# The sums over the experts of token tiles 1 and 3 move from VectorE to a tree of three additions on POOL

## What is computed

```python
logits = xt @ router_w + router_b
probs = jax.nn.softmax(logits, axis=-1)
gate = jnp.max(probs, axis=-1)
idx = jnp.argmax(probs, axis=-1)
out_all = jnp.einsum('th,ehd->ted', xt, expert_w) + expert_b[None, :, :]
e_out = jnp.take_along_axis(out_all, idx[:, None, None], axis=1)[:, 0, :]
y = gate[:, None] * e_out
...
x = _layernorm(x + _L0_ffn_ref(x, ...), axis=-1)
```

## Time and profile before

| | |
|---|---|
| median of three runs | 2217.35 us (2217.06 to 2220.44) |
| the profiled execution | 2223.95 us, of which the span is 2221.9 us |
| mean granted TensorE clock | 0.949 of full speed |
| PE / VectorE / ACT / POOL busy | 92% / 78% / 67% / 15% |
| sums over the experts on VectorE (L1470) | 32, 61.1 us |
| memsets of the attention's buffers on POOL in this stage | 20 (L640 4, L645 16), 36.7 us |

### The profile page before, as it was taken

One profiled execution on the slowest core, in us unless ns is written; L12 is line 12 of the kernel. 1 busy time (PEld: TensorE's weight loads), 2 busy tenths in 40 slices (PEclk: granted clock), 3 DMA queues, 4 the chain that ended last, 5 costly groups with the idle time before them and its releaser, 6 DMA issues.

```text
span 2221.9 us, 32029 instructions
## 1 busy us (share of the span) xinstructions
PE 2039.9 (92%) x10812; PEld 846.9 (38%) x10812; DVE 1737.5 (78%) x3501; ACT 1486.8 (67%) x2004; POOL 341.7 (15%) x385
## 2 busy tenths in 40 slices
PE   5748886999999999999999999999999999999995
PEld 2224443333333333444444444444444444443332
DVE  5856887788787877888888888888878888888884
ACT  4743453566666677777777777777777777776664
POOL 1101332000000011111111111111111111113223
PEclk9977786799999999999999999999999999999998
DMA  3001104233333355566566656556666566665630
GB/s 103 19 24 54 56 33 86 43 66 75 63 75 67 82 104 107 117 109 109 109 109 109 108 109 109 108 110 109 109 110 108 108 109 109 109 108 101 98 58 25
DMA packets 137197, 195.63 MB, mean 88 GB/s; under 512 B 20152, under 2 KB 55632, under 8 KB 137040
## 3 DMA queue, kind: packets, MB, share of 16 engines
q1 hardware_dynamic: 137040, 193.63, 45.5%
HBM read 75.45 MB, written 23.73 MB: 45 GB/s over the span
## 4 chain that ended last, share of the span: by engine, by line
PE 81%; DVE 13%; issue 4%; ACT 1%; POOL 1%; DMA 1%; DVEq 0%; POOLq 0%; SPq 0%; ACTq 0%
PE bank_s L1031 27%; PE bank_o L1069 22%; PE bank_x L1054 6%; DVE nm L1386 5%; PE bank_m L1082 3%; PE bank_x L1017 3%; PE bank_x L996 3%; PE bank_x L1004 2%; PE bank_m L1102 2%; PE bank_x L983 2%; PE bank_x L1128 2%; PE bank_s L934 1%; DVE big L1275 1%; PE bank_m L1092 1%; PE bank_m L1041 1%
## 5 line engine op out<-in xcount | busy, mean ns | idle before, releaser
L1386 DVE TENSOR_REDUCE nm<-bank_s 128x1 f32<-128x512 f32 x2048 | 1336.2, 685 | 342.3 <-PE bank_s L1031 341.4
L821 ACT ACTIVATE big<-bank_x 128x1024 f32<-128x1024 f32 x1024 | 1048.0, 1024 | 486.5 <-PE bank_x L1054 458.9
L1031 PE MATMUL bank_s<-kst,qst 62*128 62x512 f32 x2048 | 837.5, 469 | 53.1 <-DVE nm L1386 52.5
L1054 PE MATMUL bank_x<-qst,kst 64*128 64x512 f32 x2048 | 750.0, 447 | 1.6 <-ACT big L821 1.6
L1031 PEld LDWEIGHTS bank_s<-kst,qst 62*128 62x128 f32 x2048 | 358.9, 187 | 693.3 <-DVE nm L1386 609.4
L1069 PE MATMUL bank_o<-big,at 128*32 128x512 f32 x4096 | 556.4, 616 | 2.2 <-ACT big L821 2.0
L1054 PEld LDWEIGHTS bank_x<-qst,kst 64*128 64x128 f32 x2048 | 304.3, 187 | 10.2 <-issue 6.0
L605 POOL CAST at<-at 128x512 fp32r<-128x512 f32 x112 | 68.2, 609 | 1273.3 <-ACT at L752 1035.8
L607 POOL TENSOR_TENSOR at<-at 128x512 fp32r<-128x512 f32 x112 | 143.3, 1280 | 10.0
L1069 PEld LDWEIGHTS bank_o<-big,at 128*32 128x32 f32 x4096 | 81.2, 108 | 153.1 <-issue 149.2
L829 ACT ACTIVATE big<-bank_x,big 128x128 f32<-128x128 f32 x256 | 68.7, 376 | 27.3 <-issue 11.6
(11 more groups left out here) (154 smaller groups left out, 1511.4 us busy)
## 6 DMA issues: line engine op xcount, KB each, us to landing
at<-nodes_d SPq DMA_DIRECT2D x144, 256.0 KB, 5.9
kst<-at SPq DMA_DIRECT2D x288, 128.0 KB
qst<-at SPq DMA_DIRECT2D x288, 128.0 KB
nodes_d<-big SPq DMA_DIRECT2D x48, 256.0 KB, 3.1
at<-w_d SPq DMA_DIRECT2D x48, 193.0 KB, 5.8
at<-x2T_d SPq DMA_DIRECT2D x32, 256.0 KB, 4.4
kst<-at SPq DMA_DIRECT2D x128, 64.0 KB
qst<-at SPq DMA_DIRECT2D x128, 64.0 KB
```

Of the source, the lines that this page charges most:

```text
L821: act.activation(PT[:, kp, h, :, :], ring.take()[0].rearrange("p (c n) -> p c n", c=2), ACT.Exp, scale=x.c.scale).then_inc(S["c_ex"], 1)
L1031: pe.matmul(bank_s[:, n % 2, :], qst[rows, x.r, h, t * P:(t + 1) * P], kst[rows, x.r, h, :], start=True, stop=True).then_inc(S["c_s_ps"], 1)
L1054: mm = pe.matmul(sec(to, j), kst[rows, x.r, h, kc_ * P:(kc_ + 1) * P], qst[rows, x.r, h, :], start=True, stop=True)
L1386: dve.tensor_reduce(nm[:, k, at_n:at_n + 1], bank_s[:, n % 2, :], AX.X, ALU.max, negate=True).then_inc(S["c_red"], 1)
```

## The change

The sums of tiles 1 and 3 are taken from VectorE's queue. POOL does them in `scaled[1]`, in place, as a tree: 512 elements onto 512, 256 onto 256, and the last 128 onto 128 into `esum`, each addition waiting for the one before it. In POOL's queue, tile 3 of b2 comes first in an iteration, and tile 1 of b1 behind the reciprocal roots and ahead of the memsets and the split. L1412 waits for both engines' sums, and ACT's scaling of tiles 1 and 3 for POOL's. Tiles 0 and 2 stay on VectorE.

```diff
--- before.py
+++ after.py
@@ -227,8 +227,8 @@
               "ab", "ln", "sp", "mb_ps", "mb_ev", "dB_out", "link", "link2")
         names("r_", "A", "bx", "dA", "hs", "in", "out")
         names("b_", "x", "hs", "c_ps", "y", "yo_ps", "mv", "rs", "rs_link", "x1", "xT_ps", "xT_ev", "lg_ps", "lg", "ex", "mg", "mgT_ps",
-              "mgT_ev", "yb_ps", "acc", "e_ps", "sc", "red", "mv2", "rs2", "rs2_link", "x2", "x2T_ps", "x2T_ev", "out", "outT",
-              "link", "link2", "link3")
+              "mgT_ev", "yb_ps", "acc", "e_ps", "sc", "red", "red_odd", "mv2", "rs2", "rs2_link", "x2", "x2T_ps", "x2T_ev", "out", "outT",
+              "link", "link2", "link3", "tree")
         names("f_", "x3_in", "tT_ps", "tT_ev", "mv", "rs", "rs_link", "nm", "z", "mv2", "rs2", "rs2_link", "y", "out", "link", "link2", "plink")
         names("c_", "qk0", "qk1", "v0", "v1", "o0", "o1", "kh_ps", "qh_ps", "qT_ps", "v_ps", "ot_ps", "mT_ps", "wo_ps", "cT_ps", "x3T_ps",
               "kf_ev", "qf_ev", "q_ev", "v_ev", "ot_ev", "mT_ev", "pv_ev", "cT_ev", "wo_ev", "x3T_ev", "sp", "stk0", "stk1", "stk2",
@@ -622,6 +622,16 @@
                     pool.sem_inc(passed, 1)
                     in_parts(qf, qp, base + 1, S["c_sp"], 1)
 
+            def odd_sum(b, t):
+
+                of, m = scaled[1].rearrange("p e d -> p (e d)"), 2 * (2 * b + t // 2)
+                now(pool, "b_sc", b, NT, t + 1)
+                pool.tensor_tensor(of[:, 0:4 * D], of[:, 0:4 * D], of[:, 4 * D:8 * D], ALU.add).then_inc(S["b_tree"], 1)
+                pool.wait_ge(S["b_tree"], m + 2)
+                pool.tensor_tensor(of[:, 0:2 * D], of[:, 0:2 * D], of[:, 2 * D:4 * D], ALU.add).then_inc(S["b_tree"], 1)
+                pool.wait_ge(S["b_tree"], m + 3)
+                pool.tensor_tensor(esum[:, t * D:(t + 1) * D], of[:, 0:D], of[:, D:2 * D], ALU.add).then_inc(S["b_red_odd"], 1)
+
             def residual_rstd(x):
                 x = only(x, False)
                 if x is None or not x.half:
@@ -629,11 +639,14 @@
                 rstd(mv, rs0, rs, eps_ln[:, :], (S["c_mv"], x.b + 1), (S["c_plink"], x.b + 1), S["c_rs"])
 
             def body(b):
-                b2 = b - 2
+                b1, b2 = b - 1, b - 2
                 if batch(b2):
+                    odd_sum(b2, 3)
                     rstd(mvb, rsb0, rsb, eps_ln[:, :], (S["b_mv2"], b2 + 2), (S["b_rs2_link"], b2 + 2), S["b_rs2"])
                 if batch(b):
                     rstd(mva, rsa0, rsa, eps_ln[:, :], (S["b_mv"], b + 2), (S["b_rs_link"], b + 2), S["b_rs"])
+                if batch(b1):
+                    odd_sum(b1, 1)
                 if b in (2, 4, 6, 8):
                     r = b // 2 - 1
                     pool.wait_ge(S["b_y"], 2 * r + 3)
@@ -824,7 +837,7 @@
             def scale(b, t):
 
                 now(act, "b_e_ps", b, NT, t + 1)
-                need(act, S["b_red"], NT * b + t)
+                need(act, S["b_red_odd" if t % 2 else "b_red"], 2 * b + t // 2 + 1)
                 for e_ in range(NE):
                     i = act.activation(scaled[t % 2][:, e_, :], bank_x[:, t % 2, e_ * D:(e_ + 1) * D], ACT.Identity, scale=lgm[:, t, e_:e_ + 1])
                 i.then_inc(S["b_sc"], 1)
@@ -1399,15 +1412,13 @@
                     dve.tensor_scalar(nmx, mx, -1.0, None, ALU.mult).then_inc(S["b_lg"], 1)
                 if batch(b0):
                     with_d(b0, 0, A)
-                if batch(b2):
-
-                    expert_sum(b2, NT - 1)
                 if batch(b1):
                     before(dve, "b_mgT_ps", b1)
                     before(dve, "b_sc", b1, NT)
                     B.count(dve.tensor_tensor(lgm, lg, mx.unsqueeze(2).broadcast_to([P, NT, NE]), ALU.is_equal))
                 if batch(b2):
-                    now(dve, "b_red", b2, NT)
+                    now(dve, "b_red", b2, 2)
+                    now(dve, "b_red_odd", b2, 2)
                     now(dve, "b_acc", b2)
                     C.count(dve.tensor_tensor(tg[:, 1, :], tg[:, 1, :], esum, ALU.add))
                 if batch(b1):
@@ -1447,7 +1458,6 @@
                     before(dve, "b_out", b2, 16)
                     normalise(x2w, tg[:, 1, :], mvb, rsb, S["b_x2"])
                 if batch(b1):
-                    expert_sum(b1, 1)
                     now(dve, "b_yb_ps", b1)
                     before(dve, "b_x2", b1)
                     dve.tensor_tensor(tg[:, 1, :], bank_s[:, 0, :], hn, ALU.add).then_inc(S["b_acc"], 1)
```

## The result

The kernel after takes 2229.53 us (median of 5 runs, 2228.50 to 2232.94) against 2218.62 us for the kernel before (median of 5, 2217.06 to 2222.44). The ratio is 1.005, with a 95% interval of 1.0035 to 1.0064: slower by 10.9 us, or 0.5%. The profiled execution took 2229.15 us (span 2227.3).

The account below looks back on a forecast made before the run. Mostly VectorE's queue was taken to bound the expert stage, with TensorE's lower clock lengthening odd first halves. +0.6 + 9.0 - 10.4 + 6.1 = +5.3, with the clock +12.3 us, on the median 2217.35: 2229.6 us, range 2220.5 to 2238.

Parts of the forecast that it names:

- The removal: Expert stage: 16 of VectorE's 32 reductions go, 30.5 us of busy time, 30 us faster if all on the path.
- The tree: POOL's three dependent additions take 2.65 us, in latency 0.75 us longer than the reduction replaced.
- Tile 3, ordinary: First halves of b = 4 and 6: VectorE's addition of the sums waits for POOL, +0.3 us each, +0.6 together.
- Tile 3 behind the memsets: First halves of b = 3, 5, 7: tile 3's tree queues behind memsets delayed by tile 1's tree; +9.0 us.
- Tile 1 and the normalise: Second halves: VectorE reaches the normalise 1.9 us sooner, though POOL's additions hold it up; sum -10.4 us.
- two normalise instructions, second addition 0.74, the other two: end at +5.8: Second halves: the normalise, interleaved with tile 1's tree, ends 5.8 us after the mid-iteration addition.
- The end of the stage: Iterations b = 8 and 9: the last tile 1 tree delays memsets and split, and nothing covers it; +6.1 us.
- The clock: Odd iterations: a TensorE gap over 4 us lowers its clock for the second half's matmuls; +7.0 us.
- the clock holds: Rival: POOL's order binds but TensorE keeps its clock level; +5.3 us, 2222.6 us; chance 0.28.
- The step from the profiled execution to the median: Whole kernel: profiled execution lies 6.6 us above the median 2217.35, so the difference was put on the median.
- The rival on the other side: Faster rival, odd iterations: memsets end early enough not to hold tile 3's tree; -3.7 us, 2213.7 us; chance 0.04.

Follow-up runs that it names:

- end_order: The kernel after, with the last batch's tile 1 tree moved behind the memsets and the split in POOL's queue; 2227.59 us, ratio 1.0035.
- trees_last_on_dve: keep_busy with the last batch's tiles 1 and 3 summed on VectorE instead of POOL; 2199.05 us, ratio 0.9907.
- tile3_only: The kernel after with tile 1's sum back on VectorE, so only tile 3's is on POOL; 2217.95 us, ratio 0.9990.
- memsets_spread: The kernel after with POOL's blocks of five memsets taken apart and spread over the iterations; 2207.32 us, ratio 0.9946.
- keep_busy: The kernel after with spread memsets, tile 1's tree before the root, later residual addition, last split before the tree, two unread matmuls in TensorE's gap; 2202.04 us.

## Why the prediction was right, and where its steps were off

The forecast was 2229.6 us, with a range of 2220.5 to 2238. The time is 2229.53 us, on the side that was forecast (slower). The number is much closer than its steps: three terms of the sum were off by 5 to 8 us each, with different signs.

**The removal** happened as counted: 16 reductions less, and the kernel slower.

**The tree** measured 1.27 + 0.72 + 0.46 us with two gaps of 0.08, together 2.6. The forecast was 2.65.

**Tile 3, ordinary.** L1423 starts at 6.1 instead of 5.8 us (b = 2) into even iterations: +0.3, as forecast. The halves of b = 4 and 6 grew by 0.7 each, +1.3 together where +0.6 was forecast: TensorE's eight matmuls took 6.14 us in b = 4 instead of 5.40, at a granted clock of 0.60 instead of 0.68.

**Tile 3 behind the memsets.** This is the core of the forecast, and the order of the queue is as forecast: tree, memsets, tree, and VectorE standing before L1423 for 4.5 us. The wait is 4.5 us in b = 3 and 5 and 5.7 in b = 7, where 6 or more was forecast. The memsets end 15.1 us after the middle of the iteration before (230.29 - 215.20); the forecast was 15.4. L1423 came at 9.8 us into the odd iteration instead of 12.25, since the iteration itself began 2.2 us later than assumed (8.03 instead of 5.85 after the middle). From L1423 to the middle it is 6.8 us, forecast 6.6. The odd first halves are 16.7, 16.4 and 16.3, forecast 18.85, 18.85 and 17.7. Their +9.0 came out as +3.0, and most of the rest is what the next point adds: the tree waits for memsets whose end is tied to the middle of the iteration before, so a longer second half takes its time from the first half that follows.

**Tile 1 and the normalise.** Here the step "two normalise instructions, second addition 0.74, the other two: end at +5.8" fell. L1288 took 3.91 us in b = 2, 4 and 6, 2.36 in b = 3 and 5, 2.87 in b = 1 and 2.65 in b = 7, where the forecast said 2 to 2.2 in all and 3.4 nowhere. In b = 3 and 5, with the tree alone beside it, the rows are near the last stage's 2.06. In b = 1, which was taken as nothing, the second half grew by 0.6 us. In b = 2, 4 and 6 the normalise also runs into the first memset: L1288 ends at 219.27 + 3.91 = 223.18, past L653's end at 223.03, and 8.0 us after the middle instead of 5.8. I had counted the normalise as done before the memsets, though these follow the last addition with no gap. The second halves are -2.1 together, where -10.4 was forecast; 1.65 of the difference is the clock's in b = 7, below.

**The end of the stage.** +5.9 measured, +6.1 forecast, by the chain that was forecast. end_order gives 2 us of it back, trees_last_on_dve all of it.

**The clock.** The term of +7.0 is the one that fell. The forecast wanted a TensorE gap above 4 us ahead of L1177, and this to lower the level for the following second half. The gap ahead of L1177 is 0.78 us, and one of 1.31 follows ahead of L1184, because the eight matmuls ended at 10.7 us into the iteration and not at 9: their 5.48 us are more than the 3.76 of the higher level, as in before (5.40 in b = 4, 6.72 in b = 7). L1184's 16 matmuls took 2.05 us, as at the higher level, and the window of b = 3 was granted 0.85, more than the 0.76 of before. Only the second half of b = 7 runs partly at the lower level: L1204 takes 1.02 us and the four of L1141 behind it 3.24 instead of 1.88, so the half is 10.50 us instead of 8.85. That its +1.65 is near the 1.4 of the forecast is luck: the level was still the higher one behind the gap ahead of L1177 (0.73 us; L1184 took 2.05), and it was down only at L1204. So on the clock the rival "the clock holds" is what the trace shows in b = 3 and 5.

Together: the working gave +5.3 without the clock, and the stage shows +8.1, of which 1.65 are b = 7's clock, so +6.5 without it. Against the working the odd first halves gave 6.0 us less, the second halves 6.7 more without the clock, the rest 0.5 more, and the clock 5.35 less, so the stage came out 4.2 us below the forecast's +12.3. The medians differ by more than the stages, 10.9 us, which is 2.8 us that no trace here places, and before itself was 1.3 us higher in the later runs (2218.62 against 2217.35). These 4.1 us make up for the 4.2, so that the number fits to 0.1 us is chance. The step from the profiled execution to the median did not hold either: 6.6 us were taken off for it, and the profiled execution of after lies 0.4 below its median. The direction, the place and the end of the stage rest on working that held.

The rival on the other side asked for memsets that end before 5.4 to 6.6 us into the odd iteration. In after they end at 7.1 (230.29 - 223.23). For b = 5 and 7, where the bound was 6.6, it fails by only 0.4 us, and its mechanism is real: in tile3_only they end 3.4 us into b = 7 (318.00 - 314.57), and in memsets_spread they hold nothing up, and both kernels are faster than before.

**What stays open.** Why TensorE gets its higher level back sooner in some iterations than in others (eight matmuls in 3.70 to 6.72 us) is not settled, though it moves halves by over a microsecond, decided the sign in tile3_only, and the lower level comes in keep_busy with no wait of TensorE ahead of it. That the last two normalise instructions lose the port first to the additions of 256 and 128 and then to the memset is read from the start and end of the four together; no run isolated it. The 2.8 us between the stage's growth and that of the median are not located.

## What to carry to other kernels

Before work goes to an idle engine, read its queue: what stands ahead of the new instruction, what the new instruction pushes back, and who waits for its result. POOL, idle for most of the stage, had 9 us of memsets in one block, and the change cost more there than 30 us less of VectorE could bring. Taking the block apart, with no work moved between engines, was worth 10.6 us; the trees on top of that brought 4 us at most, because TensorE was the bound by then.

## What the runs showed of the hardware

POOL's additions and memsets hold VectorE's instructions up by kind. This is VectorE in after: twice beside the memsets at the start of b = 3, once with POOL idle and once beside the 512-element addition, both in b = 4:

```profile
223.10 1.91 DVE L1480 TENSOR_REDUCE big<-big 128x128 f32<-128x1024 f32 x1
...
226.97 1.58 DVE L1412 TENSOR_SCALAR big<-big 128x4 f32<-128x4 f32 x1
...
249.56 0.17 DVE L1412 TENSOR_SCALAR big<-big 128x4 f32<-128x4 f32 x1
...
250.29 0.83 DVE L1418 TENSOR_TENSOR big<-big 128x32 f32<-128x32 f32 x1
```

A `tensor_scalar` of 4 elements, 0.17 us when alone, took 1.58 us beside a memset of 1.80 that had begun 0.25 before it: it ended with the memset (228.55 and 228.52). A `tensor_tensor` of 32 elements took 0.83 us beside an addition, until 251.12, where the addition ended at 251.07. Beside a memset, as in memsets_spread (229.33 to 231.13), the same kind took no longer than the 0.19 of the earlier trace rows:

```profile
229.97 0.19 DVE L1449 TENSOR_TENSOR big<-big,rank 128x32 f32<-128x32 f32 x1
```

The reduction took its 1.91 us beside memsets, no more than anywhere. The section Who interferes with whom of the page SBUF — State Buffer in the Trainium skill says that the reduction never contends; the rows agree. What the normalise loses also depends on how closely POOL's instructions follow each other. Four normalise instructions took 2.36 us beside a tree alone, 3.42 beside memsets alone, and 3.91 beside a tree with memsets at its heels. By these figures, pieces of POOL work that follow at 0.08 us leave VectorE hardly a way in between.

The second surprise is that two matmuls an iteration whose result is thrown away, put where TensorE waited 1.2 to 1.4 us, shortened the stage by 2.8 us in the profiled executions, with all other instructions unchanged.
